# A fused attention and expert kernel on one core: fold terms moved between engines, the start-up's orders rewritten, composition ahead of the residual's last sum in some turns

## The reference, cut to what matters

```python
# x: (64, 64, 1024) float32; style: (64, 128)
def layer(x, style, w, b, mw, mb, typ):             # weights modulated per sample
    s = style @ mw.T + mb
    weight = SCALE * w * s[:, None, :, None]
    weight = weight * rsqrt(sum(weight * weight, axis=(2, 3)) + EPS)[:, :, None, None]
    # 'same': conv of 3 taps; 'upsample': transposed conv of stride 2, then a blur of 4 taps;
    # 'downsample': blur, then conv of stride 2.  plus b
def cond(x, ...):                                   # same, upsample, same, downsample
    for i, typ in enumerate(TYPES): x = layer(x, style, w[i], b[i], mw[i], mb[i], typ)
def attn(u, ...):                                   # a state-space layer
    K = ifft(c * (k00 - k01 * k10 / (1 + k11))).real        # 1024 values, from 64 complex states
    return irfft(rfft(u, 2 * L) * rfft(K, 2 * L))[..., :L] + D * u
def ffn(x, ...):                                    # 4096 rows of 1024
    base = x @ W_base.T + b_base
    w = softmax of the best 2 of 8 of (x @ W_router.T), at their experts
    return base + einsum('tr,te,eor->to', (x @ A.T) per expert, w, B) * 2
x = x + attn(cond(x, style, set 1), ...)
x = x + ffn(cond(x, style, set 2), ...)
```

## Time and profile before

| | |
|---|---|
| median of 3 runs | 1402.41 us |
| profiled execution, its own time | 1401.18 us |
| its span | 1399.3 us |
| TensorE matmul busy | 1345.8 us (96%) |
| VectorE busy | 924.9 us (66%) |
| ScalarE busy | 819.8 us (59%) |
| GpSimd busy | 790.0 us (56%) |
| chain that ended last | PE 81%, DVE 9%, POOL 4%, ACT 3%, issue 2%, DMA 1% |

### The profile page before, as it was taken

One profiled execution on the slowest core, in us unless ns is written; L12 is line 12 of the kernel. 1 busy time (PEld: TensorE's weight loads), 2 busy tenths in 40 slices (PEclk: granted clock), 3 DMA queues, 4 the chain that ended last, 5 costly groups with the idle time before them and its releaser, 6 DMA issues.

```text
span 1399.3 us, 23392 instructions
## 1 busy us (share of the span) xinstructions
PE 1345.8 (96%) x8559; PEld 1274.3 (91%) x8559; DVE 924.9 (66%) x2145; ACT 819.8 (59%) x1637; POOL 790.0 (56%) x586
## 2 busy tenths in 40 slices
PE   4679999999999999999999999999999999999998
PEld 3578899989999998899999999999999999999998
DVE  7976777777777777775565666655556555555653
ACT  4477777777887887774544444545454454544530
POOL 4367667666776676665455544554545555454542
PEclk9699999999999999999999999999999999999999
DMA  3224444444455564452444324334243332524322
GB/s 133 75 86 137 114 132 128 133 132 126 127 144 149 143 138 127 126 147 74 134 92 118 103 74 118 103 89 133 74 129 92 111 110 77 145 74 125 97 83 81
DMA packets 85988, 158.64 MB, mean 113 GB/s; under 512 B 26473, under 2 KB 47858, under 8 KB 85746
## 3 DMA queue, kind: packets, MB, share of 16 engines
q1 hardware_dynamic: 84610, 155.18, 39.6%
q10 hardware_dynamic: 1264, 1.96, 0.4%
HBM read 94.18 MB, written 33.56 MB: 91 GB/s over the span
## 4 chain that ended last, share of the span: by engine, by line
PE 81%; DVE 9%; POOL 4%; ACT 3%; issue 2%; DMA 1%; SPq 0%; DVEq 0%; POOLq 0%; ACTq 0%
PE psum L1593 25%; PE psum L1595 25%; PE psum L1594 25%; PE psum L1701 3%; DVE vm_l L1382 1%; DMA vm_f<-vv 1%; DVE vv L1376 1%; POOL xs_l L827 1%; POOL vbuf L806 1%; DVE a_f L1393 1%; POOL vbuf L802 1%; DVE xr L1418 1%; DVE a_l L1388 0%; POOL xe L235 0%; DVE xr L1422 0%
## 5 line engine op out<-in xcount | busy, mean ns | idle before, releaser
L802 POOL TENSOR_TENSOR vbuf<-vbuf 128x512 f32<-128x512 f32 x64 | 97.4, 1522 | 298.4 <-ACT vbuf L1019 298.4
L1593 PE MATMUL psum<-wt_h,u_h 128*128 128x386 f32 (+1 forms) x760 | 261.0, 343 | 0.0
L1595 PE MATMUL psum<-wt_h,u_l 128*128 128x386 f32 (+1 forms) x760 | 258.2, 340 | 0.0
L1594 PE MATMUL psum<-wt_l,u_h 128*128 128x386 f32 (+1 forms) x760 | 257.7, 339 | 0.0
L1388 DVE SCALAR_TENSOR_TENSOR a_l<-psum,tabs,a_h 128x512 fp32r<-128x512 f32 x128 | 95.7, 750 | 175.7 <-ACT a_h L987 175.7
L816 POOL TENSOR_TENSOR vm_f<-vm_f 128x512 f32<-128x512 f32 x64 | 82.7, 1292 | 176.1 <-DVE vm_l L1382 175.9
L1593 PE MATMUL psum<-a_h,vm_h 128*128 128x256 f32 x512 | 153.7, 300 | 3.1 <-ACT vbuf L1012 1.7
L1012 ACT ACTIVATE vbuf<-psum,tabs 128x512 f32<-128x512 f32 x128 | 105.1, 821 | 87.0 <-PE psum L1595 87.0
L827 POOL TENSOR_TENSOR xs_l<-xin,xs_h 128x1024 fp32r<-128x1024 f32 x64 | 141.6, 2213 | 18.9 <-ACT xs_h L973 18.9
L1024 ACT ACTIVATE u_h<-psum 128x1024 fp32r<-128x1024 f32 x64 | 65.6, 1025 | 143.7 <-PE psum L1701 143.6
L1594 PE MATMUL psum<-a_l,vm_h 128*128 128x256 f32 x512 | 146.5, 286 | 0.0
(11 more groups left out here) (297 smaller groups left out, 4019.4 us busy)
## 6 DMA issues: line engine op xcount, KB each, us to landing
vm_f<-vv SPq DMA_DIRECT2D x256, 112.0 KB, 2.6
xin<-in_x_ph_dram SPq DMA_DIRECT2D x32, 512.0 KB, 4.5
xr<-in_x_row_dram SPq DMA_DIRECT2D x32, 512.0 KB, 5.1
x1d<-xr SPq DMA_DIRECT2D x64, 256.0 KB, 3.3
xin<-x1d SPq DMA_DIRECT2D x32, 512.0 KB, 5.1
xr<-x1d SPq DMA_DIRECT2D x64, 256.0 KB, 5.7
xo<-in_b_base_dram SPq DMA_DIRECT2D x32, 512.0 KB, 3.9
out_dram<-xo SPq DMA_DIRECT2D x31, 512.0 KB, 3.0
```

The source lines that it names most:

```text
L802: G.tensor_tensor(v3[:, :, 1:H:2], v3[:, :, 1:H:2], by_odd, ALU.subtract).then_inc(v3_odd, 1)
L1593: nc.tensor.matmul(to, stat_h, mov_h, start=first_ and n == 0, stop=False, skip_group_check=True)
L1594: nc.tensor.matmul(to, stat_h, mov_l, start=False, stop=False, skip_group_check=True)
L1595: ins = nc.tensor.matmul(to, stat_l, mov_h, start=False, stop=end, skip_group_check=True)
```

## The change

- ScalarE writes all twelve terms of each fold (`terms_of`), the first six to em1 or em3, the others to spare places in xr and xo. GpSimd adds them (`folded`), after the low part of tile 0's input. VectorE's `further_terms` is gone.
- The orders of the start-up's loads on SP and ScalarE, and of `first_turns` on VectorE, ScalarE and TensorE, are changed. State sums and vectors come first on VectorE; their mask products (`state_halves`) later. On ScalarE, `rate_times_roots` comes behind m0_h. On TensorE, `pair(0, 1)` comes ahead of `transform`, `resolved` behind `edge_pe1`, `edge_pe3` ahead of `step1(2)`, `flipped` ahead of `turn(0)`.
- `blurs` is two halves of four taps; `kernel_out` stands between those of tile 1. K is sent to DRAM ahead of tile 1's vm_f DMAs and read back behind them. On ScalarE, `toeplitz` comes ahead of the pair work of turn 1.
- Edge group 0 works in PSUM in its stages 1 to 3, where it used the tile et.
- `residual` is two functions. In turns of the first half with an inserted stage, `composed1` stands between them; in other turns the order is as it was. In the second half the inserted stage goes ahead of `layer0`.
- EDGE_TURN of group 1 goes from 1 to 5, STYLE_TURN from 11 to 15, `squares(1)` from turn 1 to 3, `tap_sums(1)` from 8 to 5.

```diff
-EDGE_TURN = {1: 1, 2: 25, 3: 36}
-STYLE_TURN = 11
+EDGE_TURN = {1: 5, 2: 25, 3: 36}
+STYLE_TURN = 15
...
+    def any_inserted(i):
+        return any(edges(i, k) for k in (3, 4, 5, 6)) or any(style(i, k) for k in (-3, -2, 0, 1, 2, 3, 4, 5))
...
@@ SP
+                sp.dma_start(vec[...], d["vecs"]).then_inc(style_in, 16)
                 sp.dma_start(mwT[:, 0, :, :]..., d["mod_w"][:, 0:NL * P]).then_inc(style_in, 16)
-                sp.dma_start(vec[...], d["vecs"]).then_inc(style_in, 16)
+                sp.dma_start(cmf[:, 0, :, :]..., d["cm"][:, 0:NCM * P]).then_inc(cm_in, 16)
                 sp.dma_start(w3T[...], d["w3"]).then_inc(w3_in, 16)
-                sp.dma_start(cmf[:, 0, :, :]..., d["cm"][:, 0:NCM * P]).then_inc(cm_in, 16)
...
+                if turn_is(i, 0):
+                    to_dram()
                 if here(i + 1):
                     sp.wait_ge(blur, at(i + 1, NBLUR, NBLUR - 1))
...
                 if turn_is(i, 0):
-                    through_dram()
+                    from_dram()
@@ GpSimd
             squares(0)
+            tap_sums(0)
             mats_low(0)
-            tap_sums(0)
+            pool.wait_ge(root_ready, 1)
...
+            def folded(n, tasks):
+                pool.wait_ge(em_first, n)
+                pool.wait_ge(in_lo, 1)
+                for r in range(1, KW):
+                    for to, terms in tasks:
+                        if r < len(terms):
+                            ins = G.tensor_tensor(to, to, terms[r][2], ALU.add)
+                    if r < KW - 1:
+                        pool_link(pool, sh, ins)
+                ins.then_inc(folds, 1)
+                pool.wait_ge(folds, n)
...
                 if turn_is(i, -1):
+                    folded(1, fold1())
+                    folded(2, fold3())
                     inputs(1)
@@ ScalarE
-            def first_terms(tasks):
+            def terms_of(tasks):
                 for to, terms in tasks:
-                    ins = A(to, terms[0][0], ACT.Copy, scale=terms[0][1])
+                    for w, f, place_ in terms:
+                        ins = A(place_, w, ACT.Copy, scale=f)
                 ins.then_inc(em_first, 1)
...
             mats_high(0)
             roots_of(0)
-            rate_times_roots()
             act.wait_ge(m0_in, 16)
             A(m0_h[:, :, :, :], m0f[:, :, :, :], ACT.Copy).then_inc(mats_hi, 1)
+            rate_times_roots()
...
+                if turn_is(i, 1):
+                    toeplitz()
                 if first(i):
                     pair_sums(i)
                 if here(i):
                     pair_evacuated(i, 0)
-                if turn_is(i, 1):
-                    toeplitz()
@@ VectorE, first_turns after
                 step_reduced(); state_sum(0); state_sum(1); state_vectors()
                 styles(0); step_rate(); variances(0); step_scaled(); inverse(0); newton(0); scales(0)
                 scaled3(0); edge_scale(0); shifts(0); denominators(); composed1(0); denominators_turned()
                 through(0, 0); blurs(0); scaled3(1); edge_ve0(0); through(0, 1); resolvents()
                 through(0, 2); state_halves(); composed1(1); resolvents_scaled(); layer0(0); composed2(0)
                 transfer(); edge_ve1(0); twiddles(); scaled3(2); transposed(); blurs_begin(1)
                 kernel_out(); blurs_end(1); edge_ve2(0); edge_ve3(0); layer0(1); composed2(1); composed1(2)
@@ VectorE, body
+                if second(i - 1):
+                    inserted(i)
                 if here(i + 1):
                     layer0(i + 1)
+                if not second(i - 1):
+                    inserted(i)
...
                 if first(i - 1):
-                    residual(i - 1)
+                    residual_first(i - 1)
+                    if not any_inserted(i):
+                        residual_last(i - 1)
                 if here(i + 2):
                     composed1(i + 2)
+                if first(i - 1) and any_inserted(i):
+                    residual_last(i - 1)
@@ TensorE
                 constant(0, 2)
-                resolved()
                 pe.wait_ge(folds, 1)
                 edge_pe1(nc, pe, sh, 0, ps_p)
+                resolved()
                 pair(0, 0)
                 step2(1)
+                pair(0, 1)
                 transform()
-                pair(0, 1)
+                third(0, 0)
                 twisted()
-                third(0, 0)
                 third(0, 1)
                 second_transform()
                 edge_pe2(nc, pe, sh, 0, ps_p)
                 layer0(1)
+                pe.wait_ge(folds, 2)
+                edge_pe3(nc, pe, sh, 0, ps_p)
                 pe.wait_ge(blur, at(1, NBLUR, NBLUR - 1))
                 step1(2)
-                pe.wait_ge(folds, 2)
-                edge_pe3(nc, pe, sh, 0, ps_p)
+                flipped()
                 turn(0)
```

More of the change, by code:

```diff
@@ L1 @@
+import itertools
 from contextlib import ExitStack
@@ L328, in edge_double_first @@
             o = shift + odd
-            ins = nc.scalar.activation(sh.de[half, :, :, o:o + 7:2], sh.et[src, :, :, 0:4], ACT.Copy)
+            ins = nc.scalar.activation(sh.de[half, :, :, o:o + 7:2],
+                                       bank[src, 0:EB * 8].rearrange("p (b s n) -> p b s n", s=2, n=4), ACT.Copy)
     ins.then_inc(sh.edge_up, 1)
@@ L1194, in through @@
                     V.tensor_scalar(tabs[:, c, T_BETA4, :], x_, 2.0, None, ALU.mult).then_inc(beta_tab, 1)
-            def further_terms(tasks):
-                for r in range(1, KW):
-                    for to, terms in tasks:
-                        if r < len(terms):
-                            w, f = terms[r]
-                            last = V.scalar_tensor_tensor(out=to, in0=w, scalar=f, in1=to, op0=ALU.mult, op1=ALU.add)
-                    if r < KW - 1:
-                        link(last)
-                last.then_inc(folds, 1)
             x, n_, rr, pp = stp[:, 0:1], stp[:, 1:2], stp[:, 2:3], stp[:, 3:4]
@@ L1368, in blurs, with blurs_end, taps @@
                     ve.wait_ge(vm_in[1], 32 * g)
+                taps(g, 0, 4)
+            def blurs_end(g):
+                taps(g, 4, NBLUR)
+            def taps(g, n0, n1):
+                src = ps_step[:, 0:7 * C].rearrange("p (k c) -> p k c", c=C)
                 todo = ((0, 0, 6), (6, 2, 6), (2, 0, 6), (1, 1, 5), (4, 0, 6), (3, 1, 5), (6, 0, 0), (5, 1, 5))
-                for n, (j, k0, k1) in enumerate(todo):
+                for n, (j, k0, k1) in list(enumerate(todo))[n0:n1]:
                     to = vv[:, (k0 + j) // 2:(k1 + j) // 2 + 1, :]
@@ L1510, in first_turns, with inserted @@
                 twiddles()
-                blurs(1)
                 scaled3(2)
                 transposed()
-                ve.wait_ge(em_first, 2)
-                further_terms(fold3())
+                blurs_begin(1)
                 kernel_out()
+                blurs_end(1)
                 edge_ve2(nc, ve, sh, 0, ps_p)
+                edge_ve3(nc, ve, sh, 0, ps_p)
                 layer0(1)
                 composed2(1)
-                edge_ve3(nc, ve, sh, 0, ps_p)
                 composed1(2)
+            def inserted(i):
+                for e in edges(i, 1):
+                    if e > 1:
+                        ve.wait_ge(sh.edge_in, 64 * (e - 1))
+                    edge_scale(nc, ve, sh, e, sh.xg[:, :, :] if e > 1 else xgA[:, EB:B, :])
+                for k, stage in enumerate((edge_ve0, edge_ve1, edge_ve2, edge_ve3)):
+                    for e in edges(i, 3 + k):
+                        stage(nc, ve, sh, e, ps_late)
+                if style(i, -3):
+                    styles(1)
+                if style(i, -2):
+                    variances(1)
+                if style(i, 0):
+                    inverse(1)
+                if style(i, 1):
+                    newton(1)
+                if style(i, 2):
+                    scales(1)
+                    shifts(1)
+                for l in range(3):
+                    if style(i, 3 + l):
+                        through(1, l)
             def body(i):
```

109 lines of the change are left out of this document (52 added, 57 removed).

## The result

The changed kernel takes 1404.64 us (median; 1399.97 to 1411.38), the kernel before in the same series 1402.28 (1399.91 to 1404.02). The ratio is 1.0022, with a 95% interval of 1.0013 to 1.003. The forecast was 1389.0, with a range up to 1397. The profiled execution took 1403.94 us with a span of 1402.1, against 1401.18 and 1399.3 before: 2.8 more.

What follows compares the result with a forecast made beforehand. TensorE bounds the body, a chain over VectorE the start-up. Start-up -6.5, composition first -5.3 and second half -1.6 sum to -13.4 us, giving 1389.0 us; the 8-in-10 range is 1384.5 to 1397.

Steps and rivals of the forecast that it cites:

- Step 1: Start-up up to T: fold terms and adds leave VectorE, order changes; T moves by -1.7 us, ends -2.9 and +0.5.
- T: Mark in the start-up: end of composed2(0) on VectorE, at 49.46 us before, forecast near 47.8.
- Rival D: Start-up: GpSimd's adds and VectorE's stalls under the shared lock make T 2 us later; 1392.7 us, within the forecast's 0.66.
- Step 2: Start-up from T to TensorE's first lag matmul: new order around K column, Toeplitz read and turn 1; -4.8 us, -5.9 to -3.
- Rival A: Start-up gives nothing: T stays at 49.46 and flipped holds TensorE for the read; 1395.5 us, chance 0.16.
- C: Start-up: TensorE idles more and its clock runs at 1.2 GHz; +16.5 us, hence 1405.5, chance 0.05.
- Step 3: First-half stage turns: composition ahead of the residual's last sum removes TensorE's c_l waits; -5.3 us, 5.7 at most.
- Rival B: Stage turns give nothing: VectorE has too much to do and TensorE waits later in the turn; 1394.3 us, chance 0.10.
- Step 3, spreading: First half: inserted stages moved to later turns keep the number of such turns; nothing, with -0.5 and +0.5 as ends.
- Step 4: Second half: inserted work ahead of layer0 on VectorE removes two of four hw waits; -1.6 us, between 0 and -1.7.

Runs made afterwards that it cites:

- e5: The changed kernel with the residual's last sum ahead of composed1 everywhere and the inserted stages in their old turns: 1392.33 us, ratio 0.9933.
- e9: The kernel before with only the inserted stage put ahead of layer0 in the second half: 1399.38 us, ratio 0.9985.
- e3: The changed kernel with SP's xr load issued behind the four vm_f DMAs instead of ahead of them: 1392.23 us, ratio 0.9931.
- e1: The changed kernel with the residual's last sum ahead of composed1 again in every turn of the first half: 1394.62 us, ratio 0.9953.
- e16: The changed kernel with the xr load cut to 256 KB, one of two rows, from the second tile on: 1391.37 us, ratio 0.9926.
- e2: The kernel before with only the residual split and composed1 ahead of its last sum in turns with an inserted stage: 1413.85 us, ratio 1.0089.
- e8: The changed kernel with the inserted stages in their old turns and the xr load behind the vm_f DMAs: 1390.25 us, ratio 0.992.
- e6: The changed kernel with the last sum ahead of composed1 everywhere and the xr load behind the vm_f DMAs: 1392.51 us, ratio 0.9932.

## Why the prediction was wrong, by its own steps

**Step 1, right, and larger.** x_h of tile 0 at 22.08 (forecast 22.5 to 23), blurs(0) at 29.66 (30.1), T at 45.76 (47.8): -3.7, beyond the lower end of -2.9. The stall of 1.8 did not fall on resolvents_scaled, whose two large operations took 0.68 each. One of that kind did fall elsewhere: DVE's L1305 of 128x512 took 1.91 from 26.57, beside POOL's xs_l (24.93 to 27.93). The adds on POOL took 0.59 us each (six in 3.56) and the trace names no wait for them. Rival D is out.

**Step 2, right, and larger.** The K column left for DRAM at 57.95, T + 12.2 (forecast T + 12), `turn(0)` at 67.54 (69), `pair(1, 1)` at 73.75 (76), the first lag matmul at 81.72 (84). From T it is 35.96, where 35.2 to 36.3 was the sum. In all -8.9 in the profile against -6.5. By the medians, e5 less e9, it is -7.05, which is only 0.5 more than forecast. Rival A is out, and C too: the granted clock of the first 75 us rose from 0.82 to 0.93. The forecast had left the clock as it was; how much of the gain is the clock's is not shown.

**Step 3, wrong; this is the step that failed.** Its sentence was: "The last sum then ends 0.5 later; PE asks for it only at the next turn's stage matmul or s4, and SP's store behind it is awaited a turn later." Two things in it fail. In the ring turns the last sum starts 2.1 later, not 0.5, since it inherits c_l's wait for c_h; the prediction priced a late c_h for c_l alone. The row that it went by the earlier trace rows is from a stage turn of an edge group, where c_h was there; in such turns (28 and 29) c_l waits 0.00 after too and the last sum starts 0.5 later, as forecast. In turns 18 and 19 c_l waits for c_h for 1.0 us even with the ring open (e3), and the closed ring makes 1.6 of it. And what stands behind the sum on SP is not only a store: the load waits for the store's landing, the four vm_f DMAs stand behind the load in SP's list and land behind its 512 KB, and ACT's vm_h is asked for in the same turn. Removing either end of that (e1, e3) or half of the load (e16) takes 10 to 13 us off; adding part 3 to the kernel before (e2) costs 12.5. Rival B had the place (composition first brings nothing in stage turns) but not this mechanism, and its price was 0, not +12. No rival was a ring.

Also the size of the gain was wrong. The -5.3 was the sum of c_l waits. With the ring open it is 0.6 by the trace from turn 2 to 22, in both pairs (e5 and e8, e6 and e3), 0.2 in turns 27 to 29, and 2.1 and 0.3 by medians whose intervals overlap. In turn 29 the reason is in the rows: a vs_l wait stood right behind the c_l wait. I summed a wait without asking which one ends next on the same engine.

**Step 3, spreading, wrong by 2.** Forecast 0 with 0.5 either way; with the ring open it costs 2.3 and 2.0 by the medians of two pairs, 3.1 and 2.4 by their turns 2 to 22.

**Step 4, right.** Forecast -1.6, with -1.7 as its end; measured -2.0 alone (e9), and turns 38 and 39 gain 2.1. Two hw waits are left, as forecast.

**The sum, made again:** start-up -7, second half -2, composition first -1, spreading +2.3, the ring +10 to 12: +2 to +4. The measured medians differ by 2.4. The terms are taken from these same runs, so that they add up is no test of them.

## What to carry to other kernels

When an instruction is moved behind another, it inherits that one's wait. Follow its consumers through each queue that only issues transfers: there, what stands behind it in the list matters more than what needs it, and a period longer than the bounding engine's, with no long wait of that engine anywhere, can be a ring; the chain of waits over one turn shows whether it is. Before a sum of waits is booked as a gain, look for the next wait on the same engine and when it ends; here 1.13 us gave 0.1.

## What the runs showed of the hardware

- Median landing of the four vm_f DMAs of 112 KB, from issue, in 330 to 440 us: 4.3 us when SP issued them 0.4 to 0.6 us after one of 512 KB (changed kernel), 2.6 when 1.2 to 2.6 us after it (kernel before), 2.3 ahead of it (e3), 3.0 right behind 256 KB (e16). The load of 512 KB itself landed in 5.9 us with them right behind it and in 3.6 when issued behind them.
- DVE's stalls in edge group 0 went with the tile in SBUF: two operations of 64x192 took 2.41 us in the kernel before and 0.71 with the operand in PSUM, with POOL at work on vbuf beside both. First before, then after:

```profile
65.91 2.41 DVE L360 TENSOR_TENSOR ee<-et,tabs 64x192 f32<-64x192 f32 x2
```
```profile
59.80 0.71 DVE L366 TENSOR_TENSOR ee<-psum,tabs 64x192 f32<-64x192 f32 x2
```

- The profiled start-ups of kernels with the same start-up order as the changed one differ by up to 5 us at turn 2; what sets that is not shown.
